# Five attention stages on one core: slots without a loop, causal zeros by GpSimd, one small reciprocal per unit

## The reference

```python
# stage by stage (s = 0..7), x: (8, 512, 256)
x = x + proj(attend(ln(x), ln(x), causal=True))     # SELF0, 16 heads of 16
x = x + proj(attend(ln(x), ctx))                    # CROSS0
x = x + mlp(ln(x))                                  # MLP0, 256 -> 1024 -> 256
x = x + proj(attend(ln(x), ctx))                    # CROSS1, quantized weights
x = x + proj(attend(ln(x), ln(x), mask=given))      # SELF2
x = x + proj(attend(ln(x), ctx))                    # CROSS2
x = x + mlp(ln(x))                                  # MLP2
x = x + proj(attend(ln(x), ln(ctx), causal=True))   # SELF3, 16 heads of 64

def attend(q, k, v, causal):        # one head
    s = q @ k.T * HD ** -0.5
    if causal: s = where(tril, s, -inf)
    return softmax(s) @ v           # exp(s - rowmax) / rowsum
```

## Time and profile before

| what | us |
|---|---|
| timed runs, median of 3 (lowest, highest) | 4789.3 (4782.4, 4828.3) |
| the profiled execution, and its span | 4813.4, 4811.6 |
| PE busy | 4392.0 (91%) |
| VectorE busy | 2706.3 (56%) |
| ScalarE busy | 2289.0 (48%) |
| GpSimd busy | 1240.8 (26%) |
| first stage (SELF0), from the start to its last slot's end | about 60 to 656 |
| CROSS0 | about 656 to 1245 |

### The profile page before, as it was taken

One profiled execution on the slowest core, in us unless ns is written; L12 is line 12 of the kernel. 1 busy time (PEld: TensorE's weight loads), 2 busy tenths in 40 slices (PEclk: granted clock), 3 DMA queues, 4 the chain that ended last, 5 costly groups with the idle time before them and its releaser, 6 DMA issues. The chain is left out here.

```text
span 4811.6 us, 76408 instructions
## 1 busy us (share of the span) xinstructions
PE 4392.0 (91%) x22610; PEld 2202.8 (46%) x22610; DVE 2706.3 (56%) x6114; ACT 2289.0 (48%) x4789; POOL 1240.8 (26%) x1277
## 2 busy tenths in 40 slices
PE   5999999889896889899999999999899799999998
PEld 3555543333464333334444443333366455555555
DVE  3555677776102777787766767777400344444443
ACT  2444456555221556554444446665422355454553
POOL 1111111111221111111111111111022566666664
PEclk9888899998797889999999999998799899999999
DMA  4433434333001443433222223434100000000000
GB/s 106 64 55 59 69 73 77 66 62 59 16 0 23 89 73 62 72 58 63 47 46 46 43 47 77 81 61 74 33 16 0 27 5 10 10 10 10 10 6 10
DMA packets 115381, 218.33 MB, mean 45 GB/s; under 512 B 22320, under 2 KB 25008, under 8 KB 113328
## 3 DMA queue, kind: packets, MB, share of 16 engines
q1 hardware_dynamic: 114992, 213.79, 24.2%
HBM read 39.11 MB, written 4.19 MB: 9 GB/s over the span
## 5 line engine op out<-in xcount | busy, mean ns | idle before, releaser
L907 ACT ACTIVATE Pr<-ST 128x512 f32<-128x512 f32 (+3 forms) x2560 | 1359.1, 564 | 1370.8 <-PE ST L492 1069.9
L1089 DVE TENSOR_REDUCE mx<-MX 128x1 f32<-128x512 f32 (+3 forms) x1408 | 855.0, 629 | 503.8 <-PE MX L492 468.2
L492 PE MATMUL ST<-stk 50*128 50x512 f32 (+3 forms) x2560 | 1115.5, 486 | 16.5 <-ACT Pr L907 13.9
L492 PE MATMUL MX<-stk 48*128 48x512 f32 (+3 forms) x1760 | 773.5, 475 | 165.1 <-DMA stk<-lo 87.4
L492 PE MATMUL OV<-Pr,V 128*32 128x512 f32 (+3 forms) x5120 | 710.4, 630 | 1.5 <-ACT Pr L907 1.5
L492 PEld LDWEIGHTS MX<-stk 48*128 48x128 f32 x1760 | 329.3, 199 | 781.1 <-DVE mx L1089 414.2
L1408 POOL TENSOR_SCALAR Pr<-Pr,mx 128x128 f32<-128x128 f32 (+3 forms) x512 | 548.4, 1083 | 385.4 <-DVE mx L1227 385.4
L492 PEld LDWEIGHTS ST<-stk 50*128 50x128 f32 x2560 | 461.1, 199 | 139.7 <-ACT Pr L907 108.9
L1089 DVE TENSOR_REDUCE mx<-OV 128x1 f32<-128x512 f32 (+3 forms) x640 | 399.9, 625 | 136.3 <-PE OV L492 135.9
L1342 POOL CAST mhl<-mx 128x16 fp32r<-128x16 f32 x160 | 31.9, 199 | 1464.3 <-DVE mx L1089 1110.0
L1339 POOL TENSOR_TENSOR X<-X,brow 128x1024 f32 (+1 forms) x56 | 132.3, 2363 | 1014.7 <-DVE X L1041 1014.7
(11 more groups left out here) (134 smaller groups left out, 6766.7 us busy)
## 6 DMA issues: line engine op xcount, KB each, us to landing
stk<-hi SPq DMA_DIRECT2D x640, 128.0 KB, 3.9
stk<-lo SPq DMA_DIRECT2D x320, 128.0 KB, 4.0
misc<-misc SPq DMA_DIRECT2D x160, 128.0 KB, 3.8
sums<-misc SPq DMA_DIRECT2D x160, 128.0 KB, 4.0
misc<-in_ctx_t SPq DMA_DIRECT2D x24, 512.0 KB, 4.9
W_even<-in_w SPq DMA_DIRECT2D x4, 1024.0 KB, 5.6
W_even<-in_w SPq DMA_DIRECT2D x2, 2048.0 KB, 7.8
XH<-in_ctx_rows SPq DMA_DIRECT2D x8, 512.0 KB, 4.2
```

Of the source, the lines that this page charges most:

```text
L492: return nc.tensor.matmul(o, l, r, start=start, stop=stop)
L907: nc.scalar.activation(Pr[:, i % 2, h, q0:S], ST[h % 2][:, q0:S], ACT.Exp).then_inc(ex_done, 1)
L1089: nc.vector.tensor_reduce(m, bank[:, 0:k_n], AX.X, ALU.max).then_inc(mx_red, 1)
```

## The change

- `run_slots`: no hardware loop; all slots are written out, with the same order within a slot.
- Masks of the first stage: `add_later` and its tables (`shph`, `shpb`) are gone. VectorE reduces a causal tile with tensor_tensor_reduce (add, max) and a table `later0` in SBUF (zeros, and -1e30 above the diagonal in its last 128 columns). The scores get no mask; after the four exponentials of a step GpSimd writes zeros into the diagonal blocks of Pr, 128 x 4 x 128 (`clear`, affine_select, 8 for each unit), and `values` waits for `cleared`. To give it time, in the causal stage `values` goes from j = 1 to j = 3 of the next step, `product_out` from (0,2) to (1,0) and from (4,2) to (5,0), and `add_bias` from the even to the odd slot.
- Reciprocals: ovs has each sum on 16 partitions; the kernel now takes one of 16 only, 8 rows of 512 as 128x32 (`few`), in place of the 128 KB move to `sums`. `invert` is one reciprocal of 128x32 at (1,3). SP then writes it to a tensor in memory (`spread_rows`) and reads it back, each row to 16 partitions (`widen`, 256 KB to `sums`); the product waits for that (`spread_in`). In SP's order `spread_rows` stands ahead of `max_rows(U, half, 1)` and `widen` behind it.
- The last stage's table is made from `later0`.

```diff
@@ run_slots
-            for u in range(0 if s in JOINED else -2, 2):
+            for u in range(0 if s in JOINED else -2, UNITS if s + 1 in JOINED else UNITS + 1):
                 on = stages(u)
...
-            with eng.Fori(0, 3) as k:
-                for n in range(4):
-                    slot(4 * k + (2 + n), (2 + n) % 4, 2 * k + (1 + n // 2), k + 1, stages(2 + n))
@@ sync
                     if on["tail"]:
                         move(U - 1, 1 - half, 1, GB - 1 + half)
+                        spread_rows(U - 1, 1 - half)
                     if on["b"]:
                         max_rows(U, half, 1)
+                    if on["tail"]:
+                        widen(U - 1, 1 - half)
...
-                    sp.dma_start(sums[64 * g:64 * g + 64, half, :], ovs[1:P:2, g, :]).then_inc(ov_moved[g], 16)
+                    sp.dma_start(few[64 * g:64 * g + 64, half, :], ovs[1:P:32, g, :].rearrange("h (c n) -> h c n", n=32)).then_inc(ov_moved[g], 16)
+                def spread_rows(U, half):
+                    sp.wait_ge(recip_done, U + 1)
+                    sp.dma_start(spread[half].rearrange("h (c n) -> (h c) n", n=32), few[:, half, :]).then_inc(spread_out, 16)
+                def widen(U, half):
+                    waits(sp, (spread_out, 16 * (U + 1)), (at_ready, BASE + U))
+                    rows = spread[half].rearrange("h (a n) -> h a n", a=1).broadcast_to([2 * G, HD, S])
+                    sp.dma_start(sums[:, half, :], rows).then_inc(spread_in, 16)
@@ tensor
-                            if j == 1 and on["b"] and i > 0:
+                            if j == (3 if ATTN[s][1] else 1) and on["b"] and i > 0:
                                 values(ATTN[s][1], U, half, par, i - 1)
...
-                    last = mm(bank[:, 0:k_n], q, stk[lo_p:lo_p + 3 * HD, 8 + i, 0:k_n], True, not causal)
-                    if causal:
-                        last = add_later(bank[:, k_n - P:k_n], lo_p, C_MQ)
-                    last.then_inc(mx_full, 1)
+                    mm(bank[:, 0:k_n], q, stk[lo_p:lo_p + 3 * HD, 8 + i, 0:k_n]).then_inc(mx_full, 1)
...
-                    if causal:
-                        last = add_later(ST[h % 2][:, q0:q0 + P], lo_p, C_MK)
...
-                    pe.wait_ge(ex_done, 4 * (8 * U + i + 1))
+                    pe.wait_ge(*((cleared, 8 * U + i + 1) if causal else (ex_done, 4 * (8 * U + i + 1))))
@@ scalar
-                            if at == (0, 2) and on["tail"]:
+                            if at == ((1, 0) if causal_e else (0, 2)) and on["tail"]:
                                 product_out(U - 1, 1)
...
-                            if at == (4, 2) and on["b"]:
+                            if at == ((5, 0) if causal else (4, 2)) and on["b"]:
                                 product_out(U, 0)
@@ vector
-                            if at in ((3, 1), (3, 2), (4, 0), (4, 1)) and on["tail"]:
-                                invert(U, 1 - half, j - 1 if i == 3 else j + 2)
+                            if at == (1, 3) and on["tail"]:
+                                invert(U, 1 - half)
...
+                    elif causal:
+                        k_n = P * (qt + 1)
+                        nc.vector.tensor_tensor_reduce(bank[:, 0:k_n], bank[:, 0:k_n], later0[:, S - k_n:S], 1.0, -3.0e38,
+                                                       ALU.add, ALU.max, m).then_inc(mx_red, 1)
...
+                def invert(U, half):
+                    for g in range(2):
+                        dve.wait_ge(ov_moved[g], 32 * U)
+                    nc.vector.reciprocal(few[:, half, :], few[:, half, :]).then_inc(recip_done, 1)
@@ gpsimd
+                    if on["tail"] and ATTN[s - 1 if first else s][1]:
+                        clear(U - 1, 7)
                     if on["b"]:
                         maxima(U, half, 1)
+                    if causal and on["b"]:
+                        clear(U, 0)
                     if half == 0 and on["a"]:
                         sa, ba = a_of(s, u, b)
                         layer_norm(NB * sa + ba, xt(ba, 0, NT), la_full, JOBS * GB + 2)
+                    if causal and half == 1 and (not isinstance(u, int) or u >= 3):
+                        biased(u - 1, b, GB)
+                    if causal and on["b"]:
+                        for i in (1, 2, 3):
+                            clear(U, i)
                     if on["m"]:
                         maxima(U + 1, 1 - half, 0)
+                    if causal and on["b"]:
+                        clear(U, 4)
                     if on["tail"]:
-                        pool.wait_ge(recip_done, 4 * U)
+                        pool.wait_ge(spread_in, 16 * U)
...
+                def clear(U, i):
+                    waits(pool, (ex_done, 4 * (8 * U + i + 1)), apart=True)
+                    q0 = P * (i % 4)
+                    tile = Pr[:, i % 2, :, q0:q0 + P]
+                    nc.gpsimd.affine_select(tile, tile, [[0, G], [1, P]], ALU.is_ge, 0.0, 0, -1).then_inc(cleared, 1)
```

More of the change, by code:

```diff
@@ L96, in program @@
         mrows = sb("mrows", [P, S])
+        few = sb("few", [P, 2, 32])
+        spread = nc.dram_tensor("spread", (2, 2 * G, S), F32, kind="Internal").ap()
         cols = sb("cols", [P, N_COLS])
@@ L137, in program @@
         shp = XH[:, 0:2, :].rearrange("p a n -> p (a n)")[:, 0:3 * P]
-        half_shapes = sums[:, :, 0:3 * P]
         mask_q = W[0][:, 2048:4096].rearrange("p (t n) -> p t n", t=NT)
@@ L251, in run_slots @@
                     on.update(tail=True, op=True)
-                slot(u, u % 4, u // 2, (u // 2 + 1) // 2, on)
-            with eng.Fori(0, 3) as k:
-                for n in range(4):
-                    slot(4 * k + (2 + n), (2 + n) % 4, 2 * k + (1 + n // 2), k + 1, stages(2 + n))
-            for u in range(UNITS - 2, UNITS if s + 1 in JOINED else UNITS + 1):
-                on = stages(u)
-                if s + 1 in JOINED:
+                if s + 1 in JOINED and u >= UNITS - 2:
                     on.update(a=True, m=True)
@@ L365, in _ @@
             sp.dma_start(ident[:, :], shapes_in[:, C_ID:C_ID + P]).then_inc(consts_in, 16)
-            for lo_p in (0, 64):
-                for part in range(2):
-                    sp.dma_start(half_shapes[lo_p:lo_p + 64, part, :],
-                                 shapes_in[64 * part:64 * part + 64, :]).then_inc(half_in, 16)
             load_weights(0)
@@ L535, in slot @@
                             at = (i, j)
-                            if j == 1 and on["b"] and i > 0:
+                            if j == (3 if ATTN[s][1] else 1) and on["b"] and i > 0:
                                 values(ATTN[s][1], U, half, par, i - 1)
-                            if at == (0, 1) and on["tail"]:
-                                causal_e = ATTN[s - 1 if isinstance(u, int) and u == 0 else s][1]
+                            causal_e = ATTN[s - 1 if isinstance(u, int) and u == 0 and s in JOINED else s][1]
+                            if at == (0, 3 if causal_e else 1) and on["tail"]:
                                 values(causal_e, U - 1, 1 - half, par if half else 1 - par, 7)
@@ L605, in score_tile @@
                     last = mm(ST[h % 2][:, q0:S], k, stk[lo_p:lo_p + ROWS, head, q0:S], True,
-                              not (causal or (addmask and h in MASKED_BY_PE)))
+                              not (addmask and h in MASKED_BY_PE))
                     if addmask and h in MASKED_BY_PE:
@@ L609, in score_tile @@
                         last = mm(ST[h % 2][:, :], identr[:, :], mask_lo[:, kt, :], False, True)
-                    if causal:
-                        last = add_later(ST[h % 2][:, q0:q0 + P], lo_p, C_MK)
                     last.then_inc(st_full, 1)
-                def add_later(o, lo_p, at):
-                    rows = slice(lo_p, lo_p + 64)
-                    for part in range(2):
-                        last = mm(o, shph[rows, part, C_ID:C_ID + P], shph[rows, part, at:at + P], False, part == 1)
-                    return last
                 def values(causal, U, half, vpar, i):
@@ L1081, in max_tile @@
                     at = 32 * U + 4 * i + qt
-                    waits(dve, (mx_full, at + 1), apart=addmask)
+                    waits(dve, (mx_full, at + 1), apart=addmask or causal)
                     bank, m = MAXB[(4 * i + qt) % 3], mx[:, half, i // 4, qt, i % 4:i % 4 + 1]
@@ L1095, in add_mask @@
                                             ALU.add).then_inc(st_masked, 1)
-                def invert(U, half, j):
-                    if j == 0:
-                        dve.wait_ge(ov_moved[0], 32 * U)
-                        dve.wait_ge(ov_moved[1], 32 * U)
-                    part = sums[:, half, P * j:P * j + P]
-                    nc.vector.reciprocal(part, part).then_inc(recip_done, 1)
+                def invert(U, half):
+                    for g in range(2):
+                        dve.wait_ge(ov_moved[g], 32 * U)
```

(6 more changed lines are left out.)

34 lines of the change are left out of this document (19 added, 15 removed).

## The result

| | before | after |
|---|---|---|
| median, us (range) | 4803.6 (4775.5 to 4831.0) | 4775.0 (4759.5 to 4791.3) |
| time after / time before | 1 | 0.9938, 95% interval 0.9913 to 0.9964 |
| profiled execution, span, us | 4811.6 | 4775.8 |
| instructions | 76408 | 63412 |

The kernel became faster by 0.6%, about 30 us. The forecast was 80 us, 1.7%. The measured time (4775) lies inside the range given, but in "within 1%", which had a chance of 0.28, and not in "faster by over 1%", which had 0.62.

What follows compares the result with a forecast made beforehand. PE was taken to set the pace, held up by waits inside a slot. Terms -67 - 38 - 3 + 7 + 38 + 8 - 25 = -80 us gave a median of 4709 us, range 4630 to 4800.

Steps and rivals of the forecast that it cites:

- the term of the first stage: First attention stage, all changes but the loops: 33.7 us per unit for 35.1, times 16, -25 us (-70 to +30).
- the mask products' price of 5.3 us per unit: First stage: PE loses 128 bf16 mask matmuls with their weight loads per unit, saving 5.3 us (4.0 to 6.4).
- Loops: Two back branches in each of five attention stages go, with their stalls: -67 us (50 to 75).
- Reciprocals: Four reciprocals per unit become one of 128x32: -38 us (-15 to -58) in 48 cross units, -3 us in SELF2.
- The wait at (1,3) and slot 1: VectorE waits for the sums' move: +7 us (0 to 40) in normal cross slots, +38 (15 to 60) in slot 1s.
- Rival C: Moves land in 6.5 us rather than 4.0, losing 2.5 us in 64 slots, 160 us: 4869 us; chance 0.10.
- Tails: Ends of CROSS0 and CROSS2, where nothing hides the reciprocal, write and widening: +8 us (2 to 30).
- the copy's later place: First stage: ScalarE's last-group copy comes 2 us later, so VectorE's wait at (1,3) costs 2.75 us per unit (1 to 4).
- the clears: First stage: GpSimd's eight clears per unit at 1.56 us each, hidden except 0.75 us per unit behind layer norm.
- B: GpSimd bounds the first stage if a clear takes over 3.4 us; at 4 us, 77 us more, 4786 us; chance 0.12.
- D: The branches' stalls return in the long straight code, 67 us back: 4776 us; chance 0.08.
- A: Waits are absorbed: slot 1 loses only 15 us, first stage 1 us per unit of 5.3; -154, 4635 us; chance 0.20.

Runs made afterwards that it cites:

- the two experiments: The kernel before with only its attention loops written out, 4744.3 us; and the changed kernel with its three loops put back, 4819.2 us.
- e1: The kernel before with only the loops of the five attention stages written out; 4744.3 us, ratio 0.9873.
- e5: e4 with the first stage's masks put back on PE, as in e2; 4701.6 us, ratio 0.9778.
- e2: The changed kernel with the first stage's masks on PE and value products behind (i,1) as before; 4750.5 us, ratio 0.9896.
- e4: The changed kernel with the reciprocal behind tile (3,1) instead of (1,3), and SyncE's write of few behind the DMA of the maxima; 4710.2 us, ratio 0.9819.
- e7: e4 with VectorE's reduction plain in the first stage, without the mask table; 4722.8 us, ratio 0.9828.
- e6: e4 with the first stage's value products back behind tile (i,1) and ScalarE's copies at (0,2) and (4,2); 4679.6 us, ratio 0.9740.
- e10: e6 with the query projection of odd slots in all attention stages at (4,2) and (4,3), DMAs into stk some 3 us earlier; 4632.7 us, ratio 0.9632.
- e11: e5, all masks on PE, with the same early query projection as e10; 4633.0 us, ratio 0.9628.
- e8: e5 without the mask products of the maxima, 1024 of the 2048 mask products taken away; 4708.3 us, ratio 0.9801.

## Why the prediction was half right

What failed is the term of the first stage, in two of its steps: the mask products' price of 5.3 us per unit, and the moved value products, whose old place was given no price at all. The other terms together held within the error.

**Loops, -67 us**: right; -61 and -47 by the two experiments. From before to after the branch slots of CROSS0 and CROSS1 became 9 to 10 us shorter, about as the earlier trace rows said; from before to e1 CROSS2 gained nothing. Neither did SELF0 (577.9 and 580.4): PE's idle time there fell by 10 us (41.8 to 31.8), but the time at the low level rose from 170 to 195 us. That profile was the slowest of e1's six executions, so the latter may be chance.

**Reciprocals, -38 and -3 us**: right; -46. (SELF2 alone: 752.1 in e1 and 752.0 in e5, nothing for the -3.)

**The wait at (1,3) and slot 1, +7 and +38 us**: right in mechanism, and in sum within the error (57 measured, 22 either way, and 57 again from e2 to e5; 45 forecast), with the two terms unevenly sized. From the changed kernel to e4, slot 1 (in SELF2 slots 1 and 2) loses 10.3, 8.3, 9.0 and 5.0 us in four stages, 33 us in all, close to the forecast. The other slots of the three cross stages give back 29 us more, about 23 of them in the 36 normal slots (2 to 13), where I had 7. VectorE waits there not 1 to 1.6 us but 2.2 to 2.6 in the odd slots and 0 to 2.8 in the even ones. In the slot of the earlier trace rows, after, the issue on SyncE and the reciprocal:

```profile
983.01 0.61 SPq L420 DMA_DIRECT2D few<-misc  x1
...
987.65 0.35 DVE L1097 RECIPROCAL few<-few 128x32 f32<-128x32 f32 x1 [2.37 <-DMA few<-misc]
```

From issue to use it took 4.6 us, not the 4.0 of the median, and the price was not small: the 36 normal slots wait 67 us and lose 23, in one profile of each kernel. Rival C (2.5 us in 64 slots, 160 us) had the size of the wait in the odd slots but not its price; most of it is still covered.

**Tails, +8 us**: the interval with the end of CROSS0 and the MLP grew by 1.4 us, that from CROSS2's last copy to the end of the program by 0.3, and PE's wait for GpSimd's product at the two ends from 17.8 to 20.6 us. Too dear, small.

**First stage, -25 us**: wrong, +20 (19 either way), so it lost what it was to gain. By its own steps: the copy's later place, +2.75 us per unit for the wait in front of the reciprocal, cost nothing that can be seen (3 us in the stage between the changed kernel and e4); VectorE's table nothing that can be told (e7); the clears 0.63 us for the 1.56 assumed, and 0.7 us of PE in the stage for the 12 forecast. Two steps failed. The step that moved the value products by one pair of tiles was priced only by what comes behind them, the copy, and not by what they had covered: in their old place they gave ScalarE the time to free two score banks. Without that time PE waits 42 us for them, and putting the products back gives 38 us (e6 against e4), 28 in the changed kernel itself. And the price of the mask products, 5.3 us per unit from the earlier trace rows or 85 us in the stage, was taken at the full clock as a sum of work, with only 16 us to come back as a wait for stk. Of the 85 us 18 came through (e6 against e5, 22 either way), and that wait grew by only 3 us (21.6 to 24.8). The rest is an estimate from one profile each: 23 us more of idle time, 23 to 32 us for the lower level of the clock, and some 12 to 20 us that I can't assign. The prediction had named the granted clock of this stage as the thing that could prove it wrong, but gave it no term and no rival.

**Rivals.** B (clears over 3.4 us) fell by a factor of five. By the Trainium skill (GPSIMD Engine Reference, section 3.1, Elementwise — side-by-side cycle accounting) the selection would take an estimated 5.1 us if it branched per element. The trace shows 0.63, so that rule doesn't apply to it. D fell with e1. A and C were wrong in size on either side. The one that came true, a loss in the first stage by a new wait of PE for ScalarE together with the clock, wasn't among them.

## What to carry to other kernels

When an instruction group is moved, price what it covered in its old place, not only what waits for it in the new one: filler between two uses of a double-buffered bank is worth up to the round trip that it hides. Work taken off an engine whose clock follows its load is not worth its busy time; look first at how long the stage stands at the lower level, and count on a part. And a wait that needs a DMA belongs late in an in-order queue: the same reciprocal at (3,1) instead of (1,3), with the value products back in place and the query projection some 3 us earlier, gives 4633 us (e10, ratio 0.9632), 147 us faster than the changed kernel, while the same without any of the mask change (e11, 0.9628) is as fast.

## What the runs showed of the hardware

GpSimd's selection over 128x512 takes 634 ns, half of its two-input product of the same size (1.26 to 1.27 us). VectorE's sum with a table and maximum in one costs the kernel nothing that can be told against a plain maximum (e4 and e7 are 4 us apart, 23 either way). A write of 16 KB to memory lands in 1.4 us, nearly as late as one of 128 KB. Adding products to PE raised its granted clock: 0.80 to 0.86 over the first stage with 940 recorded products more (e8 to e5), and 0.78 to 0.90 with 1944 more (e10 to e11), both at equal or shorter time. And the scatter between executions of one kernel goes with this clock: 0.36 us of time for each us at the lower level over 12 executions of the changed kernel, correlation 0.99.
